# Two layers of cross-attention on one core: the keys' last columns of both layers as one block

## The reference

```python
# layer 0                                         # layer 1
text = ctx[:, :77]; ip = ctx[:, 77:]              text = ctx[:, :-4]; ip = ctx[:, -4:]
q = x @ Wq.T                                      q = x @ W_q
k = text @ Wk.T;  k_ip = ip @ Wk_ip.T             k_t = text @ W_k;  k_ip = ip @ W_k_ip
v = text @ Wv.T;  v_ip = ip @ Wv_ip.T             v_t = text @ W_v;  v_ip = ip @ W_v_ip
out = attend(q, k, v) + attend(q, k_ip, v_ip)     probs_t = softmax(q @ k_t * 0.25)
x = out @ Wo.T + bo + x                           qsem = l2norm(probs_t @ text)
                                                  fused = q @ k_ip * 0.25 + 0.5 * qsem @ l2norm(ip)
                                                  probs_ip = softmax(fused) * mask
                                                  out = probs_t @ v_t + probs_ip @ v_ip
                                                  x = out @ W_out + b_out + x
```

## Time and profile before

| | us |
|---|---|
| median of 3 runs | 1678.19 (1675.70 to 1682.73) |
| the profiled execution, whole time | 1678.24 |
| its span | 1676.4 |
| PE busy / DVE busy / ACT busy | 1580.9 / 1280.6 / 1096.5 |
| mean granted clock of TensorE | 0.983 of full speed |

### The profile page before, as it was taken

One profiled execution on the slowest core, in us unless ns is written; L12 is line 12 of the kernel. 1 busy time (PEld: TensorE's weight loads), 2 busy tenths in 40 slices (PEclk: granted clock), 3 DMA queues, 4 the chain that ended last, 5 costly groups with the idle time before them and its releaser, 6 DMA issues.

```text
span 1676.4 us, 25931 instructions
## 1 busy us (share of the span) xinstructions
PE 1580.9 (94%) x7968; PEld 1190.7 (71%) x7968; DVE 1280.6 (76%) x3552; ACT 1096.5 (65%) x2323; POOL 560.3 (33%) x1313
## 2 busy tenths in 40 slices
PE   6899999999999999999999999999999999999993
PEld 3565489999456459999756537999965654899981
DVE  3698279898789538899779835999887982798985
ACT  1697278886388537888438926888726872788860
POOL 0243034443044214444214403444403430344430
PEclk9899999999999999999999999999999999999995
DMA  9010310010311221001121122000030113000100
GB/s 316 22 44 16 113 56 25 20 36 1 114 34 39 78 69 54 20 20 31 51 73 40 45 90 75 20 21 24 22 113 23 41 31 113 15 25 20 36 1 16
DMA packets 65953, 83.90 MB, mean 50 GB/s; under 512 B 29188, under 2 KB 36628, under 8 KB 65816
## 3 DMA queue, kind: packets, MB, share of 16 engines
q1 hardware_dynamic: 63144, 77.11, 15.6%
q10 hardware_dynamic: 2672, 5.13, 0.9%
HBM read 41.49 MB, written 34.10 MB: 45 GB/s over the span
## 4 chain that ended last, share of the span: by engine, by line
PE 75%; DVE 10%; ACT 8%; issue 3%; DMA 1%; SPq 1%; POOL 1%; POOLq 0%; ACTq 0%; DVEq 0%
PE ps_w L1006 41%; PE ps_s L1006 16%; PE ps_t L1006 11%; PE ps_b L1006 5%; ACT probs L577 3%; DVE probsT_low L758 3%; DVE row_max L822 2%; PE ps_b L1140 2%; ACT probsT_high L558 2%; ACT probsT L566 2%; DVE probs L846 1%; DVE stat L831 1%; ACT probs L592 1%; PE ps_m L1006 1%; DMA slots<-out_all 1%
## 5 line engine op out<-in xcount | busy, mean ns | idle before, releaser
L558 ACT ACTIVATE probsT_high<-ps_t 128x512 fp32r<-128x512 f32 x640 | 384.3, 600 | 101.6 <-PE ps_t L1006 101.5
L758 DVE TENSOR_TENSOR probsT_low<-probsT,probsT_high 128x512 fp32r<-128x512 f32 x560 | 385.0, 688 | 39.4 <-ACT probsT L566 34.6
L566 ACT ACTIVATE probsT<-ps_t 128x512 f32<-128x512 f32 x640 | 387.2, 605 | 0.0
L1006 PE MATMUL ps_w<-gram,probsT_high 128*128 128x416 f32 (+2 forms) x1280 | 383.1, 310 | 0.0
L1006 PE MATMUL ps_w<-gram_low,probsT_high 128*128 128x384 f32 (+2 forms) x1280 | 352.1, 304 | 0.0
L485 POOL TENSOR_SCALAR exp_bias<-row_max 128x1 f32<-128x1 f32 x320 | 136.8, 428 | 544.7 <-DVE row_max L822 544.7
L592 ACT ACTIVATE probs<-ps_s,exp_bias 128x508 f32<-128x508 f32 x320 | 220.9, 691 | 130.6 <-POOL exp_bias L485 89.6
L1006 PE MATMUL ps_s<-slots 96*128 96x512 f32 x640 | 281.1, 481 | 21.2 <-DVE row_max L773 9.7
L1006 PE MATMUL ps_t<-slots 98*128 98x512 f32 x640 | 252.2, 415 | 1.8 <-ACT probsT L566 1.4
L1006 PEld LDWEIGHTS ps_w<-gram_low,probsT_high 128*128 128x128 f32 (+1 forms) x1280 | 242.0, 189 | 6.5
L1006 PE MATMUL ps_w<-gram,probsT_low 128*128 128x400 f32 (+2 forms) x1280 | 246.1, 314 | 0.0
(11 more groups left out here) (168 smaller groups left out, 2100.9 us busy)
## 6 DMA issues: line engine op xcount, KB each, us to landing
slots<-parts SPq DMA_DIRECT2D x128, 192.0 KB, 3.3
parts<-probsT_high SPq DMA_DIRECT2D x16, 512.0 KB, 4.0
parts<-probsT_high SPq DMA_DIRECT2D x24, 256.0 KB, 3.7
parts<-probsT_low SPq DMA_DIRECT2D x8, 512.0 KB, 3.4
parts<-x_sb SPq DMA_DIRECT2D x8, 512.0 KB, 3.9
slots<-probsT_high SPq DMA_DIRECT2D x24, 128.0 KB, 3.3
parts<-probsT_low SPq DMA_DIRECT2D x12, 256.0 KB, 3.6
ctx_sb<-in_ctxT ACTq DMA_DIRECT2D x3, 1024.0 KB, 5.5
```

Of the source, the lines that this page charges most:

```text
L558: nc.scalar.activation(probsT_high[1 - par][:, t, :], ps_t[:, t % 2, :], ACT.Exp, scale=SCALE)
L566: nc.scalar.activation(probsT[:, t, :], ps_t[:, t % 2, :], ACT.Exp, scale=SCALE).then_inc(pt_block[l], 1)
L758: nc.vector.tensor_tensor(probsT_low[1 - par][:, t, :], probsT[:, t, :], probsT_high[1 - par][:, t, :].bitcast(F32), ALU.subtract).then_in ...
L1006: return nc.tensor.matmul(out, lhsT, rhs, start=start, stop=stop)
```

## The change

The last 64 columns of layer 0's keys and the last 64 of layer 1's become one block of 128, made as the third block of layer 0's keys, at the place of that block. On the host the matrices are put together: `wk0` and `wki0` become 384 columns wide (their own 320 and layer 1's last 64 of `W_k`), `wk1` and `wki1` 256, and a new `wkt` holds 128 columns of image weights (`W_k_ip`) of both layers. The joint block has three context ranges, as the two layers change weights at different columns: 0 to 77, 77 to 508, 508 to 512.

The block's lower 64 rows are stored to layer 1's scratch in the stage of layer 0's keys. Layer 1's key stage has two blocks. `JOBS` has one entry less, and the ring is turned by one, so that all later jobs keep their banks. The first loads of layer 0's keys are cut by columns: 128 columns of both matrices first, the rest and `wkt` behind x and the queries' weights, with an own semaphore that PE waits for at the second block of the first batch. To make room, `half_high` shares memory with `v0_sb` and `vip` with `fused`, with one new wait each on ScalarE and VectorE.

```diff
+C2 = 2 * P
+KEYS1 = 2
+BLOCKS = {"k0": CBN, "q0": CBN, "k1": KEYS1, "q1": CBN}
+ROWS = {(name, m): P if (name, m) == ("k0", CBN - 1) else CB[m] for name in BLOCKS for m in range(BLOCKS[name])}
-STORES = CBN * 2 * 16
+STORES = {"k0": (CBN + 1) * 2 * 16, "q0": CBN * 2 * 16, "k1": KEYS1 * 2 * 16, "q1": CBN * 2 * 16}
...
-    [("k1", m, "D") for m in range(CBN)]
+    [("k1", m, "D") for m in range(KEYS1)]
...
-        vip = sb("vip", [IPN, C])
-        half_high = sb("half_high", [P, SC, P], F32R)
+        half_high = v0_sb[:, 1:1 + TB, :, :].rearrange("p t h d -> p (t h d)")[:, 0:SC * P].rearrange("p (c k) -> p c k", c=SC).bitcast(F32R)
+        vip = fused[0:IPN, :, :].rearrange("r n i -> r (n i)")
...
-            return ring[RING_NEXT[name, m] if (name, m) in RING_NEXT else JOB[name, m] % RING]
+            return ring[RING_NEXT[name, m] if (name, m) in RING_NEXT else (JOB[name, m] + 1) % RING]
...
-            load_big("k0", wk0, weights0_in["k"])
-            load_big("ki0", wki0, weights0_in["k"])
+            def load_keys(cols, there):
+                for n, src in (("k0", wk0), ("ki0", wki0)):
+                    sp.dma_start(w_big[n][:, :, cols], src[:, cols].rearrange("(k p) n -> p k n", p=P)).then_inc(there, 16)
+
+            load_keys(slice(0, P), weights0_in["k"])
             load_x(sp, 0)
             load_small("q0", wq0, weights0_in["q"])
+            load_keys(slice(P, C2 + P), weights0_in["rest"])
+            sp.dma_start(w_kt[:, :, :], wkt.rearrange("(k p) n -> p k n", p=P)).then_inc(weights0_in["rest"], 16)
             load_big("v0", wv0, weights0_in["v"])
...
                     store(name, m)
+                    if ROWS[name, m] > CB[m]:
+                        store(name, m, "k1", CB[m])
...
                 wait_job(act, b, "v0i", t)
+                if t == 0 and b is not FIRST:
+                    act.wait_ge(less_half, HEADS * (b + 1))
...
+                dve.wait_ge(vip_stored, 16 * (b + 1))
                 link(b, nc.vector.tensor_tensor(fused[:, :, :], o1[:, :, A1:A1 + IPN], rn.to_broadcast([P, nd, IPN]), ALU.mult))
...
+            def last_keys(b):
+
+                out, cols = free_bank(b, "k0", CBN - 1), slice(C2, C2 + P)
+                over_e(out[:, 0:TEXT0], lambda e: w_big["k0"][:, e, cols], lambda e: ctx_sb[:, e, 0:TEXT0])
+                over_e(out[:, TEXT0:TEXT1], lambda e: w_big["ki0"][:, e, cols], lambda e: ctx_sb[:, e, TEXT0:TEXT1])
+                over_e(out[:, TEXT1:T], lambda e: w_kt[:, e, :], lambda e: ctx_sb[:, e, TEXT1:T]).then_inc(job_done, 1)
...
                 for m in range(CBN):
-                    keys(b, "k0", "ki0", TEXT0, (m,))
+                    if m == 1 and b is FIRST:
+                        pe.wait_ge(weights0_in["rest"], 48)
+                    if m < CBN - 1:
+                        keys(b, "k0", "ki0", TEXT0, (m,))
+                    else:
+                        last_keys(b)
...
-                keys(b, "k1", "ki1", TEXT1)
+                keys(b, "k1", "ki1", TEXT1, range(KEYS1))
...
+    whole = {name: given[name] for name in ("wk0", "wki0", "wk1", "wki1")}
+    both = 2 * P
+    given["wk0"] = np.concatenate([whole["wk0"], whole["wk1"][:, both:]], axis=1)
+    given["wki0"] = np.concatenate([whole["wki0"], whole["wk1"][:, both:]], axis=1)
+    given["wkt"] = np.concatenate([whole["wki0"][:, both:], whole["wki1"][:, both:]], axis=1)
+    given["wk1"], given["wki1"] = whole["wk1"][:, 0:both], whole["wki1"][:, 0:both]
```

More of the change, by code:

```diff
@@ L90 @@
 PER_B = {e: FREED_BY.count(e) for e in "AD"}
-HIGHS = [(name, m) for name in ("k1", "q1") for m in range(CBN)] + [(name, m) for m in range(CBN) for name in ("k0", "q0")]
+HIGHS1 = [(name, m) for name in ("k1", "q1") for m in range(BLOCKS[name])]
+HIGHS = HIGHS1 + [(name, m) for m in range(CBN) for name in ("k0", "q0")]
 FIRST = "first"
@@ L183, in build @@
         late.update({job: late_ring[i % len(late_ring)] for i, job in enumerate(BETWEEN)})
-        weights0_in = {n: sem(f"weights0_in_{n}") for n in "kqv"}
+        weights0_in = {n: sem(f"weights0_in_{n}") for n in ("k", "rest", "q", "v")}
         weights_in = sem("weights_in")
@@ L347, in load_biases, with store @@
                 sp.dma_start(mask_sb[:, :], mask).then_inc(weights_in, 16)
-            def store(name, m):
-                rows = scratch[name].rearrange("i g d k s -> (g d k) i s")[P * m:P * m + CB[m], :, :]
+            def store(name, m, to=None, first=0):
+                to = to or name
+                rows = scratch[to].rearrange("i g d k s -> (g d k) i s")[P * m:P * m + CB[m], :, :]
                 for part, at in enumerate(ROW_TARGETS[name[0]]):
-                    src = parts[name][part].bitcast(F32)[0:CB[m], m, :]
+                    src = parts[name][part].bitcast(F32)[first:first + CB[m], m, :]
                     dst = rows[:, at[0]:at[-1] + 1:max(at[-1] - at[0], 1), :]
@@ L381, in split_and_loaded @@
                 for name in names:
-                    sp.wait_ge(stored[name], STORES * (batch + 1))
+                    sp.wait_ge(stored[name], STORES[name] * (batch + 1))
                 sp.sem_inc(passed, 1)
@@ L512, in gram_ready @@
                 def gram_ready():
[L514 removed]
+                    pool.wait_ge(stored["q1"], STORES["q1"] * (b + 1))
                     wait_freed(pool, b, "v1", TB - 1)
@@ L544, in high @@
                 wait_job(act, b, name, m)
-                nc.scalar.activation(parts[name][0][0:CB[m], m, :], bank(name, m)[0:CB[m], :],
-                                     ACT.Copy).then_inc(high_in, 1)
+                rows = ROWS[name, m]
+                nc.scalar.activation(parts[name][0][0:rows, m, :], bank(name, m)[0:rows, :], ACT.Copy).then_inc(high_in, 1)
             def shift(b, n, k):
@@ L570, in step0 @@
                 if transposed and not use:
-                    act.wait_ge(stored["k0"], STORES * (b + 1))
+                    act.wait_ge(stored["k0"], STORES["k0"] * (b + 1))
                 if transposed:
@@ L607, in step1 @@
                     gram_rows(b, 2)
-                    act.wait_ge(stored["k1"], STORES * (b + 1))
+                    act.wait_ge(stored["k1"], STORES["k1"] * (b + 1))
                 for c in range(SC):
@@ L664, in highs @@
             def highs(b, name):
-                for m in range(CBN):
+                for m in range(BLOCKS[name]):
                     high(b, name, m)
@@ L677, in context_done @@
                     if ahead:
-                        act.wait_ge(stored["q1"], STORES * (b + 1))
+                        act.wait_ge(stored["q1"], STORES["q1"] * (b + 1))
                         load_ctx(act, b + 1)
@@ L691, in batch @@
                 if ahead:
-                    for name, m in HIGHS[2 * CBN + 2:]:
+                    for name, m in HIGHS[len(HIGHS1) + 2:]:
                         high(b, name, m)
@@ L699, in batch @@
                     fill0(step0, b + 1, b)
-            for name, m in HIGHS[2 * CBN:]:
+            for name, m in HIGHS[len(HIGHS1):]:
                 high(FIRST, name, m)
@@ L789, in step0 @@
                 if transposed and not use:
-                    dve.wait_ge(stored["q0"], STORES * (b + 1))
+                    dve.wait_ge(stored["q0"], STORES["q0"] * (b + 1))
                 if transposed:
@@ L1239, in ip_context, with keys @@
                     .then_inc(job_done, 1)
-            def keys(b, name, split, text, ms=range(CBN)):
+            def keys(b, name, split, text, ms):
                 for m in ms:
-                    out, cols = free_bank(b, name, m), slice(m * P, m * P + CB[m])
-                    over_e(out[0:CB[m], 0:text], lambda e: w_big[name][:, e, cols], lambda e: ctx_sb[:, e, 0:text])
-                    over_e(out[0:CB[m], text:T], lambda e: w_big[split][:, e, cols], lambda e: ctx_sb[:, e, text:T])\
-                        .then_inc(job_done, 1)
+                    out, cols = free_bank(b, name, m), slice(m * P, m * P + P)
+                    over_e(out[:, 0:text], lambda e: w_big[name][:, e, cols], lambda e: ctx_sb[:, e, 0:text])
+                    over_e(out[:, text:T], lambda e: w_big[split][:, e, cols], lambda e: ctx_sb[:, e, text:T]).then_inc(job_done, 1)
+            def last_keys(b):
[3 more added lines that the diff above has]
+                over_e(out[:, TEXT1:T], lambda e: w_kt[:, e, :], lambda e: ctx_sb[:, e, TEXT1:T]).then_inc(job_done, 1)
             def by_channels(b, name, w, src, ms=range(CBN)):
@@ L1337 @@
         "mask": np.asarray(fside_S_0).reshape(SC, P).T,
+        "wkt": np.asarray(L1_xattn_W_k_ip)[:, 0:P],
         "wq0": np.asarray(L0_xattn_Wq).T,
```

14 lines of the change are left out of this document (8 added, 6 removed).

## The result

The changed kernel takes 1666.67 us, the median of 6 runs (1664.62 to 1669.61), against 1679.82 us for the kernel before, run beside it (6 runs, 1674.95 to 1682.73): a ratio of 0.9924, 95% interval 0.991 to 0.9937. It is faster by 0.76%, and the predicted 1667.4 us lies 0.7 us above the measured median. The profiled execution took 1668.66 us (span 1666.7), 9.6 us less than the profiled execution of before (1678.24), where the sum had said 10.8.

What follows compares the result with a forecast made beforehand. PE was taken as the bound, except at the start, where the first slot loads wait behind SP's queue. -15.88 + 3.60 + 1.5 = -10.8 us on the profiled 1678.24 gave 1667.4 us, range 1662 to 1674.

Steps and rivals of the forecast that it cites:

- The narrow block: Layer 1's key stage: dropping its third block saves PE 3.97 us in each of four batches, -15.88 us.
- The last block of the first layer's keys: Layer 0's key stage: the full block with three ranges costs PE 1.20 us more, three times, +3.60 us.
- the third range: Last block of layer 0's keys: four 4-column products in two passes, priced at 0.88 us by an earlier group.
- the widening: Last block of layer 0's keys, 64 to 128 rows: a full two-range block takes 3.85 us for 3.50.
- VectorE's last heads stay hidden: Behind layer 0's last key block: heads finish near 448.2 us, PE asks at 449.67, 1.5 us to spare.
- The start: Program start: added bytes and packets ahead of the first slot loads delay the first scores, +1.5 us.
- the three further issues cost SP nothing: Program start: SP is through at 6.97 us and waits for VectorE until 8.77, so added issues cost 0.
- The clock: Output products at batch starts: PE's clock may fall or hold, from -2.8 to +2.2 us, outside the sum.
- A: Program start: packets rule, first slots land 5.3 us later instead of 1.5; 1671.3 us, chance 0.18.
- B: Start costs nothing and output products run at full clock, -15.1 us; 1663.2 us, chance 0.18.
- C: Layer 1's heads: a slot load behind the removed block takes the whole gain, +5.1 us; 1683.3 us, chance 0.04.
- D: First batch's second block: waiting for the remaining keys holds PE; about the forecast's time, chance 0.60 together with the forecast.

Runs made afterwards that it cites:

- e2: Changed kernel, its full last block of layer 0's keys with two context ranges, the four-column third left out: 1664.42 us, 0.9903 of the kernel before.
- e3: Changed kernel with the first loads of layer 0's keys undivided, same bytes in 1024 packets less: 1662.82 us, 0.9893 of the kernel before.
- e4: Kernel before with only the first key loads divided by columns, no joint block: 1679.54 us against 1679.08, ratio 0.9999.
- e5: Changed kernel with the second layer's and output's weights issued one by one behind the first batch's slot loads: 1655.94 us, 0.9874 of the kernel before.
- e6: Changed kernel with later weights issued behind the first slot loads and layer 0's first key loads undivided: 1658.95 us, 0.9899 of the kernel before.
- e8: Changed kernel with later weights behind the first slot loads and second scores ahead of the last image-value block: 1656.84 us, 0.9883 of the kernel before.
- e9: Changed kernel with 27 unused products on PE in the last batch's idle time: 1664.1 us, 0.9911 of the kernel before.
- e10: Changed kernel with later weights behind first slots, second scores ahead of the last value block, and 27 unused products: 1650.9 us, 0.9835 of the kernel before.

## Why the prediction was right

**The narrow block.** -3.97 x 4 was the forecast, -4.06 x 4 = -16.24 the measurement. The method, start to start on the bound engine, was right; that the heads would be 2.36 us ahead was right too (2.28). The 0.09 more comes from the seam: the second block, followed by transposes, takes 171.26 - 166.96 = 4.30 us where it took 4.37 followed by a third block, and from the transposes to the output product are 2.28 us for 2.30.

**The last block of the first layer's keys.** +1.20 x 3 forecast, +1.27 x 3 measured. The sum was right within 6%, with two parts off against each other: the third range is 0.76 in place (forecast 0.85) and the widening 0.51 (forecast 0.35, e2). Start to start the third range does take 432.86 - 431.98 = 0.88 us, as the row of the other stage had it. The forecast that VectorE's last heads stay hidden held: its last chain ends at 446.2 us, the transposes begin at 447.66.

**The start.** +1.5 forecast, +1.31 measured, but in part by another way than the forecast's. I priced the added bytes and packets, and took for granted that the three further issues cost SP nothing, because SP had 1.8 us of waiting for VectorE. That step failed: the three take 0.59, 0.91 and 1.05 us and push the values' weights back, whose two issues then last 2.71 and 2.06 us; at 8.77 us SP is still in the first of these, the slack is gone, and SP gets to the first slot loads 1.78 us later. I had read that the chain goes over SP, and then priced only what stands in its queue. In the changed kernel SP is through with the later weights 6.4 us after the first part is ready, and 1.11 of the 1.31 us stand in its issuing, 0.20 in the load's own time. Whether it is late by its own three issues, or because a full queue of more bytes holds its issues up, no run tells, so it is in part luck that the sum came near. The added matrix, bytes and packets, makes 0.50 us (e3), the division 0.16 to 0.81 (e4, e3), each uncertain by about 0.5. A term that the sum left out: behind PE's idle time the values ran at the lower clock, 1.84 us against the undivided loads. Against the kernel before it shows as nearly nothing (second scores at 50.04 us for 48.57, +1.47 after +1.31), because there the values ran partly at the lower clock already (4.01 us for 2.32).

**The clock.** Left to chance, -2.8 to +2.2 us, and it came to +0.46: batch 1 gained, batch 2 lost, batch 3 lost a little. That the same code may fall either way was right, and it holds beyond what I looked at: at the end of the kernel it is worth 4.5 us, and it is the likely cause of the two groups of runs of one and the same kernel. The profiled executions, 1678.24 and 1668.66, both had the low clock there (5.78 us), so that their difference of 9.6 is clean of the end's clock. The medians, 13.15 apart, aren't: before, the profiled execution lies 1.6 below the median, and after, 2.0 above. The median hit the forecast to 0.7 us partly for that reason, which is luck; on the profiled execution the forecast was 1.2 us too low, 1668.66 for 1667.4.

**The rivals.** A (packets) is refuted by e4 and e3. B's start at no cost did not happen, +1.31. C (a cover) did not either: the slot load behind the stage moved with PE (189.02 us for 191.72, 3.28 for 3.27 long), and the stage's whole gain is still there at the next stage (-2.69 before, -2.14 after the heads of batch 0, -6.55 and -6.61 in batch 1); the 0.55 us lost once has no cause that I could show. D did not happen: PE has no idle time between its first product and 29.40 us, so the wait for the rest of the keys holds nothing up.

## What to carry to other kernels

Here a narrow block on the bound engine costs nearly what a full one does (3.50 for 4.01 us, e2), so folding two into one gains what the difference of starts says (3.97 forecast, 4.06 found); a range of a few columns is then the price, 0.76 us for eight 128-column weight loads. Before dividing a load to start the bound engine sooner, follow the chain to the first work that it can't do without: here the division was worth nothing or less (e4, e3) until loads needed later were issued behind those needed now (about 8 us, e5), and about 2 us afterwards (e6). An engine that issues loads in order is itself a queue: compare when the data for a load are ready and when its issue begins (16.65 and 23.18 us here). When a gain in the middle doesn't reach the end (e8), look at how long the same last instructions take in both traces before looking for a new wait.

## What the hardware showed that I had not expected

After 24.6 us without work PE's transposes run in every kernel at the lower clock, 1.2 GHz (1.09 us for 0.63), but the products that follow 3.5 us later run at either level, 5.78 or 3.04 us for the same six. The granted clock shows it: first the changed kernel over the idle stretch and the six products, then e5 over its first products (start:end, length, PE busy and count, granted clock, DMA share, GB/s):
```profile
1621.90:1646.40 24.50, 0.00 (x0) 0.56 0.00 0
1649.92:1655.60 5.68, 5.67 (x6) 0.50 0.00 0
```
```profile
1641.80:1647.50 5.70, 5.70 (x12) 1.00 0.14 49
```
With the idle time filled with unused products, both traces have full clock at the end (e9, e10). The Trainium skill (TensorE: Matmul & The Clock Gate, "What's actually happening") says of the slow products at a kernel's start that their number varies from run to run and that they cost below 1% of a typical span. In size the traces agree, for slow products late in a kernel: 4.5 us at the end and up to 1.7 at each of three first output products, 9.6 us together, are 0.6% of the span. But the whole change is worth 0.76%, and beside that they aren't small.

The second surprise is how little packets cost at the start (2.5 to 13 ns each, if all of the difference is theirs), and that a backlog shows not only as late landings but, as I read it, as long issues on the engine that issues: 2.71 us for the first matrix of values, where the second layer's of the same size took 0.59 at 18.86 us. Late landings: the changed kernel's slot loads take 3.3 us from issue to landing in the median, the releasing one at the start 9.03.
